# Turning the third batch's attention rows later in the first batch of the MLP's first layer

## What is computed

```python
h = layernorm(x) * (1 + ca) + sa
x = x + ga * attention(h)                  # 16 heads, causal, then W_proj (512 x 512)
h = layernorm(x) * (1 + cb) + sb
y = relu(h @ W1.T + b1)                    # 512 -> 1024
y = relu(y @ W2.T + b2)                    # 1024 -> 1024
x = x + gb * (y @ W3.T + b3)               # 1024 -> 512
```

## Time and profile before

| | us |
|---|---|
| median of 3 runs | 1472.52 |
| lowest, highest | 1472.03, 1473.81 |
| the profiled execution | 1473.96 |
| its span, first to last instruction | 1472.20 |
| PE busy in the span | 1429.3 (97%) |
| DVE busy | 1109.3 (75%) |
| ACT busy | 811.0 (55%) |

### The profile page before, as it was taken

How to read it: one execution, slowest core, us unless ns; L and a number is a source line. 1 busy time by engine, 2 the same in 40 slices (tenths; PEclk the granted TensorE clock), 3 DMA queues, 4 the chain that set the end, 5 groups by cost and what they waited for, 6 DMA issues and landing times. The chain is left out here.

```text
span 1472.2 us, 30356 instructions
## 1 busy us (share of the span) xinstructions
PE 1429.3 (97%) x12048; PEld 1282.3 (87%) x12048; DVE 1109.3 (75%) x1955; ACT 811.0 (55%) x1468; POOL 447.0 (30%) x450
## 2 busy tenths in 40 slices
PE   8989999999999999999899999989999999999998
PEld 4578888787888888887799999989999999999998
DVE  4588777787778787778976766897766667688887
ACT  3266666666666766677655555574434333454331
POOL 3276666667666766666200000000000000000000
PEclk9999999999999999999999999999999999999999
DMA  8534454434444444455444444445755566589885
GB/s 279 151 96 102 98 128 102 112 93 116 95 109 99 113 102 95 109 123 157 154 152 164 169 172 173 181 158 193 274 199 191 203 222 243 196 313 303 302 295 179
DMA packets 126894, 247.15 MB, mean 168 GB/s; under 512 B 13977, under 2 KB 36505, under 8 KB 126753
## 3 DMA queue, kind: packets, MB, share of 16 engines
q1 hardware_dynamic: 122720, 241.56, 52.6%
q10 hardware_dynamic: 4032, 3.66, 0.8%
HBM read 114.58 MB, written 79.72 MB: 132 GB/s over the span
## 5 line engine op out<-in xcount | busy, mean ns | idle before, releaser
L572 POOL TENSOR_TENSOR prob_lo<-prob,prob_hi 128x512 f16<-128x512 f32 x256 | 301.5, 1181 | 149.8 <-ACT prob L705 148.9
L698 ACT ACTIVATE prob_hi<-key_score 128x512 f16<-128x512 f32 x320 | 191.3, 598 | 131.9 <-PE key_score L1039 130.6
L2502 PE MATMUL sum_b<-op,w 128*128 128x256 f32 x1728 | 218.0, 284 | 1.6 <-DVE op L2004 1.3
L926 PE MATMUL lin<-h_parts,wqk 128*128 128x512 f32 x768 | 215.7, 404 | 3.5 <-POOL h_parts L532 2.8
L2502 PEld LDWEIGHTS sum_b<-op,w 128*128 128x128 f32 x1728 | 211.4, 192 | 2.7 <-DVE op L2004 1.5
L880 DVE TENSOR_REDUCE row_max<-score 128x1 f32<-128x512 f32 (+2 forms) x384 | 180.2, 498 | 22.9 <-PE score L1026 22.7
L705 ACT ACTIVATE prob<-key_score 128x512 f32<-128x512 f32 x320 | 190.7, 596 | 0.0
L926 PEld LDWEIGHTS lin<-h_parts,wqk 128*128 128x128 f32 x768 | 140.4, 192 | 32.6 <-DVE h_parts L753 4.7
L1026 PE MATMUL score<-stack 96*128 96x512 f32 (+3 forms) x512 | 154.8, 363 | 0.0
L2502 PE MATMUL sum_e<-op,w 128*128 128x256 f32 x1152 | 146.8, 284 | 3.3 <-issue 1.4
L2502 PE MATMUL sum_a<-op,w 128*128 128x256 f32 x1152 | 145.5, 284 | 0.9 <-issue 0.8
(11 more groups left out here) (166 smaller groups left out, 2590.4 us busy)
## 6 DMA issues: line engine op xcount, KB each, us to landing
stack<-qk_parts SPq DMA_DIRECT2D x384, 128.0 KB, 2.4
late_op_whole<-y_dram SPq DMA_DIRECT2D x40, 512.0 KB, 5.0
y_dram<-u_c SPq DMA_DIRECT2D x32, 512.0 KB, 3.2
blk<-y_dram SPq DMA_DIRECT2D x32, 512.0 KB, 4.1
y_dram<-y_sum SPq DMA_DIRECT2D x24, 512.0 KB, 3.1
x_tiles<-x SPq DMA_DIRECT2D x32, 256.0 KB, 3.3
attn_dram<-o_rows SPq DMA_DIRECT2D x32, 256.0 KB, 2.5
x_dram<-res_tiles SPq DMA_DIRECT2D x8, 1024.0 KB, 8.5
```

The lines of the kernel that those rows point to most:

```text
L572: nc.gpsimd.tensor_tensor(prob_lo[:, key[1] % 2, u, :], prob[:, u, :], prob_hi[:, key[1] % 2, u, :], ALU.subtract).then_inc(lo_pool, 1)
L698: nc.scalar.activation(prob_hi[:, q % 2, u, :], bank[:], ACT.Exp, scale=SOFTMAX_SCALE, bias=P_SHIFT)
L926: mm = nc.tensor.matmul(lin_bank_of((QK, f))[:], wqk[:, wl, c, at:at + P], h[:, hl, c, :], start=(c == 0 and k == 0), stop=(c == NC_ - 1 a ...
L2502: mm = nc.tensor.matmul(dst, w[:, wl, c, cols], data[:, dl, c, :], start=begin, stop=end, skip_group_check=again)
```

## The change

Batch 0 gets a table of its own, `AUX_AT_FIRST`. Its four groups of the third batch (batch 2) move from the third and fourth product (s = 2 and 3) to behind the fifth, sixth and seventh (s = 4, 5, 6), in between the four groups of normalised rows, which move by one m step in part. ACT gets the order `first_rows()` for batch 0; DVE's four `turned_lo` move behind `lo(0, 5)`.

```diff
+AUX_AT_FIRST = {(0, 3): [(PROJ, 1, 2)], (1, 3): [(PROJ, 1, 3)], (4, 3): [(TURNED, 2, 0)], (5, 0): [(TURNED, 2, 1)],
+                (5, 1): [(ROWS, 1, 0)], (5, 3): [(ROWS, 1, 1)], (6, 0): [(TURNED, 2, 2)], (6, 1): [(ROWS, 1, 2)],
+                (6, 2): [(TURNED, 2, 3)], (6, 3): [(ROWS, 1, 3), (PROJ, 2, 0), (PROJ, 2, 1)]}
...
 def aux_at(k, s, m):
-    return [(kind, k + ahead, i) for kind, ahead, i in AUX_AT.get((s, m), []) if k + ahead < B]
+    at = AUX_AT if k else AUX_AT_FIRST
+    return [(kind, k + ahead, i) for kind, ahead, i in at.get((s, m), []) if k + ahead < B]
...
+            if n == 0:
+                first_rows()
+                return
...
+        def first_rows():
+            hi(0, 5)
+            normalise(1)
+            turned_hi(2, 0)
+            hi(0, 6)
+            turned_hi(2, 1)
+            relu(0, C11)
+            modulate(1, 0)
+            modulate(1, 1)
+            turned_hi(2, 2)
+            hi(1, 0)
+            modulate(1, 2)
+            turned_hi(2, 3)
+            modulate(1, 3)
+            relu(0, C22)
+            relu(0, C21)
+            hi(1, 1)
...
-            rows, turn, last = k + 1 < B, k + 2 < B, k == B - 1
+            rows, turn, last = k + 1 < B, 0 < k < B - 2, k == B - 1
...
+            if n == 0:
+                turned_lo(2, 0)
             lo(n, 6)
+            if n == 0:
+                turned_lo(2, 1)
...
             first_op_sum(n + 1)
+            if n == 0:
+                turned_lo(2, 2)
+                turned_lo(2, 3)
```

## The result

| | before | after |
|---|---|---|
| median of 20 runs, us | 1472.28 | 1474.83 |
| lowest, highest | 1470.40, 1476.11 | 1472.15, 1479.33 |
| profiled execution, its span | 1473.96, 1472.2 | 1472.86, 1471.1 |

The ratio after to before is 1.0016, with a 95% interval of 1.0008 to 1.0023: **2.4 us slower** (1.2 to 3.4), or 0.16%. The forecast was 0.4 us faster. The single profiled execution of after is faster than that of before all the same, and that says nothing on the change: its third product starts at 721.45, 3.15 us earlier than before's 724.60, ahead of all that the change touches. Each execution has pieces of half clock elsewhere too, at a cost of about 1.7 us each and in changing number: before's had five ahead of that point, after's two. The comparison has to be made by distances inside the changed stretch and behind it.

A forecast was written before the change was run, and what follows sets the result against it. TensorE was busy 97% of the span, with DVE's list bounding the sixth product. Its 1.73 us gain shrank to about 0.7, plus 0.24 at the projection, then to 0.4 by the last link: 1472.52 to 1472.1 us, range 1471.0 to 1474.2.

The forecast's parts named there:

- the cost of the seven groups: Batch 0, sixth and seventh product: three turned groups join four of rows at 0.36 us each; 8.50 us in all.
- three `turned` operations less: DVE's list ahead of batch 0's sixth product: 1.80 us shorter, so that product starts 1.73 us earlier.
- The waits: TensorE idle ahead of batch 0's fifth product, its sixth, and batch 2's projection: 0.75, 2.5 and 0.5 to 0.6 us.
- The first group of rows: Batch 0: its bank comes free after ACT's first cast, held behind `normalise`, with 0.6 us of room left.
- The small loss of about 0.1 us in DVE's list: `minus_means` waits for POOL with only `third_sum` as cover; 0.05 to 0.1 us lost.
- the last link: Batch 2's projection waits 0.5 to 0.6 us for its fourth turned group, so starts only 0.35 to 0.4 us earlier.
- Free: SP's `load_at(3)`, issued at 744.8 instead of 735.0, and stores held behind it were said to cost nothing.
- rival 1: Clock drops in the merged 2.5 us gap ahead of the sixth product: 1.7 us lost, 1473.8 us; chance 0.20.
- late casts: ACT holds the first cast behind `normalise`, delaying groups of rows: 0.5 to 1.5 us, most likely 1472.9; chance 0.14.
- all waits gone: DVE further ahead than its list says; three waits and the projection's 0.24 us vanish: 1468.9 us; chance 0.04.
- a free last link: Hand-over to batch 2's projection quicker than its rows: 0.95 us gained, 1471.6 us; chance 0.12, shared with other gains.

The follow-up runs named there:

- stores first: Changed kernel with SP issuing the store of batch 1's rows and the C11 store ahead of the load waiting for the fourth turned group; ratio to before 1.0007.
- w6 later: Changed kernel with the low part of the seventh product's weights moved on DVE behind the sixth product's operand; ratio to before 1.0005.
- longer gap: Kernel before with two extra DVE operations ahead of the low part of the sixth product's weights; ratio to before 1.0017.
- c: Third of three further profiled executions of the changed kernel, nothing altered; 1476.20 us.

## Why the prediction was wrong

The balance of the five profiled executions of the changed kernel: half clock in 4 of 5, with A on average 1.48 us longer than before where it fell, so 0.8 x 1.48 = 1.2 us; B on average 35.78 - 34.81 = 1.0 us. Together 2.2 us, against 2.4 us (1.2 to 3.4) measured. The share of 4 in 5 is read from few executions (4 in 6 with that of the stores first, where the gap is the same), and so the split between clock and stores is rough. The forecast had 0.4 us of gain, and the sign came out the other way. Two steps of the prediction made the loss: it held the later load on SP to be free, and its sum took the clock loss at nothing. A third, the cost of the seven groups, took away the gain.

**Right.** DVE's list bounds the sixth product, and three `turned` operations less bring it forward: it starts 12.66 us behind the third product, predicted 12.55, before 14.28. The waits were 0.80, 2.41 and 0.34 us, predicted 0.75, 2.5 and 0.5 to 0.6; the last was reckoned by distance from the end of TensorE's own list, and by that it was 745.26 - 744.69 = 0.57 us in the execution without half clock. The first group of rows did not wait for ACT. The small loss of about 0.1 us in DVE's list came, but not for POOL: `third_sum` covered that (1.21 us between the two starts, no idle time). It lay between `add_rows` and the statistics, which read its result and had a `turned` between them before; they now start 0.72 us apart instead of 0.60.

**Mis-sized: the seven groups.** "Sixth and seventh product with seven groups take 8.50 us". From the sixth product to the end of its own list TensorE took 735.90 to 744.69 in the execution without half clock, 8.8 us:

```profile
735.90 0.95 PE L2536 MATMUL sum_e<-op,w 128*128 128x256 f32 x6 [2.40 <-DVE w L2095]
736.68 0.60 PE L2452 MATMUL aux<-ident,attn_tiles 128*128 128x128 f32 x4
737.04 0.96 PE L2536 MATMUL sum_e<-op,w 128*128 128x256 f32 x6
...
744.33 0.60 PE L2479 MATMUL aux<-ident,norm_tiles 128*128 128x128 f32 x4
745.26 5.73 PE L2464 MATMUL aux<-wproj,turned 128*128 128x512 f32 x24 [0.34 <-DVE turned L1928]
```

The end, 744.69, is the start of the last group and its 0.36 us. Where a product is cut behind six matmuls, these take 0.80 us and not 0.75, at six places. Five of them lie ahead of the fourth turned group, which comes some 0.25 us later by them, and with it the last link. That and the 0.1 us of DVE ate the 0.4 us: A is 22.02 against 22.00. The gain of 1.6 us at the sixth product was given back in full by the three groups that moved behind it, the cuts that they make and the last link.

**Wrong step: "Free".** I priced SP's later load by its own reader, batch 1's first turned group, and that reader indeed never waited. The store of batch 1's rows and those of C11, C22 and C21, which it holds back, I named, but I gave them no landing times: the room of over 5 us was reckoned for ACT's relu operations of C22 and C21. The store of C12 and the sum that waits for it I did not name at all. Moved from 10.4 to 22.0 us behind the third product, the load and the store of batch 1's rows met the four stores and the next load, and the last store took 7.9 us to land instead of 2.6. What ended last was a wait of DVE for a buffer to come free.

**Wrong step: the clock at nothing; rival 1 happened.** Place and price were right (1.70 us of clock each time, of which some 1.46 arrive in A). The chance was too low by what came: 0.20 given, 4 of 5 seen. I had set the idle 2 us at full clock at 96 us against it. One such row does not bound the risk: the same gap of 2.4 us goes both ways in different executions of one kernel. The very place of that row shows it too. The gap there is 2.64 us long, no kernel here changes it, and half clock stands behind it in 4 of the 14 profiled executions, as in the one of w6 later:

```profile
96.00:98.00 2.00, 1.37 (x21) 1.36 (x22) 1.96 (x4) 1.24 (x2) 1.72 (x3) 0.86 0.58 133
98.00:100.00 2.00, 2.00 (x15) 1.93 (x14) 1.25 (x3) 1.06 (x2) 2.00 (x2) 0.50 0.59 135
```

The Trainium skill (TensorE: Matmul & The Clock Gate, "HAM oscillation — how this bites in real kernels") has the rule that I set beside the rows: an idle gap between bursts sends the clock back to half rate. The trace agrees in 4 of 5 executions of the changed kernel and not in the fifth; the waits in that section's own example are longer than 2.4 us, so it did not settle this case either. Whether transposes beside a gap count as part of it, no run here separates. The range reached to 1474.2 for this rival alone; both losses together lie above it, at 1474.83.

The rivals of late casts, of all waits gone and of a free last link did not come. The times given for the late casts did not follow from their price either: 0.5 to 1.5 us on top of 1472.1 make 1472.6 to 1473.6, and not 1472.3 to 1473.3.

## What to carry to other kernels

When waits of TensorE are moved, look at their pieces and not at their sum: before had 3.34 us in three pieces without loss of clock, after 3.55 us in three pieces of which one is 2.41 us, and that one cost another 1.5 us in 4 of 5 profiled executions. When a step moves that a DMA waits for, price everything behind that DMA in its queue, with landing times taken where several transfers are under way, up to the buffers whose reuse waits for a store. And where one engine's list bounds another, first take out of that list what the next consumer does not need: here one operation of 1.13 us stood ahead of the operand that was waited for.

## What the runs showed of the hardware

- A loss of clock comes in equal portions: all pieces of half clock in the changed stretch, in four executions of the changed kernel and one of the kernel with the longer gap, sum to 1.70 to 1.72 us of full clock. Elsewhere in the traces they do too, but for 3.42 us near 20 us in four executions and for the fall at the kernel's end.
- Whether it falls is not settled by the gap alone. With one gap of 2.4 us it fell in 4 of 5 profiled executions of the changed kernel and not in the one with the stores first; with gaps up to 1.5 us never in the stretch, in one execution each of seven kernels; with 2.84 us in the one there is. It can start inside the gap (after) or more than 1 us behind it (c). Outside the stretch, a gap of 2.60 to 2.66 us near 97 us, the same in all 14 profiled executions, had half clock behind it in 4 of them, and one of 1.7 us near 338 us in 6. What decides that stays open.
- Stores of 512 KB landed in 2.6 to 3.0 us with little else under way, in 4.6 us with two transfers of 1024 KB under way (before's C11), and in 7.9 to 10.4 us with seven other transfers issued in 11 us.
- Cutting a row of 12 matmuls in two costs TensorE about 0.1 us (2 x 0.80 instead of 1.50), beside the 0.35 us of the transposes put in.
